# GAT score split into a linear and a relu part in a graph-network kernel: source shares as extra table columns, pair sums read from PSUM

## The reference

```
xl = x @ Wl + bl                       # source side
xr = x @ Wr + br                       # destination side
e = leaky_relu(xl[src] + xr[dst], 0.2) # per edge, 128 numbers
score = einsum('ehc,hc->eh', e, att)   # per edge and head
alpha = softmax of score over the edges of each dst
out[dst] = sum of alpha * xl[src]
```

## Time and profile before

| What | us |
|---|---|
| three runs | 7042.58, 7057.05, 7068.73 |
| median | 7057.05 |
| profiled execution, first to last instruction (span) | 7063.2 |
| first GAT pass, its 832 gathers begin and end within | 2300 to 3440 |
| second GAT pass | 3443 to 4700 |

### The profile page before, as it was taken

The page is one execution under the profiler, slowest core; times in us unless marked ns, Lnnn a source line. Parts: engine busy times, 40 slices in busy tenths (PEclk is TensorE's granted clock), DMA queues, the critical chain, the costliest instruction groups (busy, mean ns, idle before and its releaser), DMA issues. The chain is left out here.

```text
span 7063.2 us, 92210 instructions
## 1 busy us (share of the span) xinstructions
PE 4905.6 (69%) x26319; PEld 4070.8 (58%) x26319; DVE 5007.0 (71%) x14623; ACT 1757.9 (25%) x5241; POOL 4834.6 (68%) x5008
## 2 busy tenths in 40 slices
PE   2555555677666677777688888876888886676766
PEld 2444443566655455555466666656777775666665
DVE  4444433777776688888588878856877774788886
ACT  2333332222222122222122222221222221121121
POOL 3777776777775777777477666627777772777774
PEclk7666676777777888888788888877888886777776
DMA  4544445666665444444454454536766774666665
GB/s 135 170 152 163 160 153 159 206 215 211 209 214 147 149 156 154 152 159 160 106 165 161 153 163 156 170 105 223 245 228 227 238 230 120 222 217 221 226 223 139
DMA packets 408009, 1264.30 MB, mean 179 GB/s; under 512 B 128774, under 2 KB 189958, under 8 KB 321110
## 3 DMA queue, kind: packets, MB, share of 16 engines
q1 hardware_dynamic: 200000, 760.63, 30.1%
q0 software_dynamic: 200240, 492.90, 24.7%
q10 hardware_dynamic: 7270, 4.88, 0.2%
HBM read 1081.15 MB, written 176.88 MB: 178 GB/s over the span
## 5 line engine op out<-in xcount | busy, mean ns | idle before, releaser
L755 POOL DMA_INDIRECT gathered_rows<-table_l,arena x3056 | 2981.2, 976 | 1230.3 <-issue 906.8
L1313 PE MATMUL ps<-weighted_rows,onehot 128*128 128x136 f32 (+2 forms) x8320 | 1547.6, 342 | 646.0 <-DVE acc L1165 641.3
L1313 PEld LDWEIGHTS ps<-weighted_rows,onehot 128*128 128x128 f32 x8320 | 1360.0, 241 | 818.3 <-DVE weighted_rows L1154 382.7
L1280 PEld LDWEIGHTS ps<-dst_side,onehot_t 128*128 128x128 f32 x8320 | 1312.3, 234 | 384.1 <-issue 327.0
L755 POOL DMA_INDIRECT gathered_rows<-table_l,src_rel_edges x1120 | 1067.8, 953 | 601.3 <-issue 329.0
L1280 PE MATMUL ps<-dst_side,onehot_t 128*128 x8320 | 1390.1, 322 | 84.6 <-issue 43.3
L1165 DVE TENSOR_TENSOR acc<-acc,ps 128x136 f32 (+2 forms) x4160 | 1186.4, 285 | 121.3 <-PE ps L1313 39.5
L1277 PE MATMUL ps<-gathered_rows,ident 128*128 128x512 f32 x832 | 556.3, 756 | 266.1 <-DMA gathered_rows<-table_l,arena 256.9
L1087 DVE TENSOR_REDUCE scores<-products 128x16 f32<-128x512 f32 (+2 forms) x1040 | 709.0, 682 | 13.3
L878 PE MATMUL ps<-gathered_rows,onehot 128*128 128x128 f32 x1664 | 346.7, 374 | 471.6 <-ACT gathered_rows L815 470.5
L755 POOL DMA_INDIRECT arena<-table_l,src_rel_edges x544 | 517.6, 952 | 178.3 <-issue 159.8
(11 more groups left out here) (314 smaller groups left out, 6233.5 us busy)
## 6 DMA issues: line engine op xcount, KB each, us to landing
onehot_t<-onehots_turned SPq DMA_DIRECT2D x260, 1024.0 KB
onehot<-onehots SPq DMA_DIRECT2D x260, 1024.0 KB, 5.4
onehots<-onehot SPq DMA_DIRECT2D x52, 1024.0 KB, 6.8
onehots_turned<-onehot_t SPq DMA_DIRECT2D x52, 1024.0 KB, 4.3
table_l<-arena SPq DMA_DIRECT2D x50, 1024.0 KB
gathered_rows<-table_l,arena POOLq DMA_INDIRECT x3056, 2.5
segment_flags_sb<-segment_flags SPq DMA_DIRECT2D x1300, 8.2 KB
arena<-type_mask_rows SPq DMA_DIRECT2D x75, 256.0 KB
```

Of the source, the lines that this page charges most:

```text
L755: pool.indirect_dma_start(out=home(v, t // GC)[:, t % GC, :], out_offset=None, in_=table, in_offset=bass.IndirectOffsetOnAxis(ap=index[:, ...
L1280: ins = nc.tensor.matmul(ps[:, BZ + k, g * P:(g + 1) * P], e.ohT[:, u, t * P:(t + 1) * P], kRows[:, bass.ds(bs[t % 8], D)], start=not gat, ...
L1313: ins = nc.tensor.matmul(ps[:, BP + n % 3, at:at + PW], e.oh[:, u, t, :], exvT[:, t, :], start=True, stop=True)
```

## The change

leaky_relu(z, 0.2) is 0.2 z + 0.8 relu(z). The linear part of a score is a sum of a source share and a destination share; the latter is the same for all edges of a destination and leaves the softmax as it is. The source share, 0.2 att·xl per node and head, is made once per node (`linear_share`), and stored in columns 128 to 131 of the table: a row of a GAT table grows from 512 to 528 bytes. Att is scaled by 0.8 once (`scale_att`). In a slot, VectorE now takes max(z, 0) * att straight out of PSUM in one instruction; ScalarE's four copies and VectorE's four multiplications by att go. ScalarE copies the group's linear shares out of the gathered rows (`keep_linear`), and TensorE adds them when it turns the scores: two accumulating matmuls against the identity in place of one transposition. `own_shares` loses one operation over 128 columns and gains one over 1 or 4. The gathered rows' buffers and the projected rows (`xlW`) get the wider pitch.

```diff
+TW = D + 4
-        t2_d = [table(f"table_l2_{n}", (NPAD, D)) for n in range(2)]
+        t2_d = [table(f"table_l2_{n}", (NPAD, TW)) for n in range(2)]
-        rows = sb("gathered_rows", [P, 2, GT * 2 * D])
+        rows = sb("gathered_rows", [P, 2, GT * 2 * TW])
+        linS = sb("linear_shares", [P, GT * 4])
...
-            def keep_pair_sums(s, j):
+            def keep_linear(s, w):
+
                 if gat:
-                    c, k = J * s + j, j % 2
-                    e.z_ready.wait(act, a_no, c + 1)
-                    if not (static(s, 1) and j < 2):
-
-                        e.score_ready.wait(act, a_no, c - 1)
-                    nc.scalar.activation(e.prod[:, k, :], ps[:, BZ + k, :], ACT.Copy).then_inc(e.zc_ready.sem, 1)
+                    e.z_ready.wait(act, a_no, J * (s + 1))
+                    at = (w % buffers) * GT * width
+                    rows = e.rflat[:, at:at + GT * width].rearrange("p (t c) -> p c t", c=width)
+                    nc.scalar.activation(e.linS[:, 0:L].rearrange("p (h t) -> p h t", t=GT), rows[:, D:D + H, :], ACT.Copy)\
+                        .then_inc(e.linear_kept.sem, 1)
...
                 if gat:
-                    e.zc_ready.wait(dve, gat_no, c + 1)
-                    V.scalar_tensor_tensor(e.prod[:, k, :], ps[:, BZ + k, :], 0.2, e.prod[:, k, :], ALU.mult, ALU.max)\
-                        .then_inc(e.prod_ready.sem, 1)
-                    return
...
+                    ins = V.scalar_tensor_tensor(out, z, 0.0, att.unsqueeze(1).to_broadcast([P, GC, D]), ALU.max, ALU.mult)
...
-            def weight_att(s, j):
-                if gat:
-                    e.prod_ready.wait(dve, a_no, J * s + j + 1)
-                    pr = e.prod[:, j % 2, :].rearrange("p (g d) -> p g d", d=D)
-                    V.tensor_tensor(pr, pr, att.unsqueeze(1).to_broadcast([P, GC, D]), ALU.mult).then_inc(e.att_step.sem, 1)
...
-                    nc.tensor.matmul(ps[:, BZ + k, :], e.ident[:, :], home(v, j).rearrange("p g d -> p (g d)"), start=True, stop=False)
+                    nc.tensor.matmul(ps[:, BZ + k, :].rearrange("p (g d) -> p g d", d=D), e.ident[:, :], home(v, j)[:, :, 0:D],
+                                     start=True, stop=False)
...
-                nc.tensor.transpose(scoresP, e.sc[:, 0:L], e.ident[:, :]).then_inc(e.turned_ready.sem, 1)
+                if gat:
+                    nc.tensor.matmul(scoresP, e.sc[:, 0:L], e.ident[:, :], start=True, stop=False)
+                    e.linear_kept.wait(pe, gat_no, s + 1)
+                    nc.tensor.matmul(scoresP, e.linS[:, 0:L], e.ident[:, :], start=False, stop=True).then_inc(e.turned_ready.sem, 1)
+                else:
+                    nc.tensor.transpose(scoresP, e.sc[:, 0:L], e.ident[:, :]).then_inc(e.turned_ready.sem, 1)
...
+    def scale_att(self, dve):
+
+        n = self.layer
+        att = self.e.vecs[:, (n - 1) * D:n * D]
+        dve.wait_ge(self.S["w"], 16 * 5)
+        self.chain.step(dve, self.nc.vector.tensor_scalar(att, att, 0.8, None, ALU.mult))
+
+    def linear_share(self, dve, k, t, H):
+
+        e, S, V = self.e, self.S, self.nc.vector
+        n = self.layer
+        att, own = e.vecs[:, (n - 1) * D:n * D], e.xlW[:, k, D:D + H]
+        dve.wait_ge(S["own_made"], k + 1)
+        if H == 1:
+            ins = V.scalar_tensor_tensor(t, e.xlN[:, k, :], 0.25, att, ALU.mult, ALU.mult, accum_out=own)
+        else:
+            self.chain.step(dve, V.scalar_tensor_tensor(t, e.xlN[:, k, :], 0.25, att, ALU.mult, ALU.mult))
+            ins = V.tensor_reduce(own, t.rearrange("p (h c) -> p h c", h=H), AX, ALU.add)
+        ins.then_inc(S["share_made"], 1)
+        dve.wait_ge(S["share_made"], k + 1)
...
-        sp.wait_ge(S["own_made"], k + 1)
+        sp.wait_ge(S["share_made"], k + 1)
...
-        sp.dma_start(t2[bass.ds(b, 1), :, :].rearrange("b p d -> p (b d)"), e.xlN[:, k, :]).then_inc(S["written"], 16)
+        sp.dma_start(t2[bass.ds(b, 1), :, :].rearrange("b p d -> p (b d)"), e.xlW[:, k, :]).then_inc(S["written"], 16)
...
+            elif d == 15:
+                self.linear_share(dve, k, self.junk, 4)
...
     c.step(dve, V.tensor_tensor(t, e.xlN[:, k, :], e.kN[:, k, :], ALU.add))
-    c.step(dve, V.scalar_tensor_tensor(t, t, 0.2, t, ALU.mult, ALU.max))
     if H == 1:
-        c.step(dve, V.scalar_tensor_tensor(t, t, 1.0, att, ALU.mult, ALU.mult, accum_out=own))
+        c.step(dve, V.scalar_tensor_tensor(t, t, 0.0, att, ALU.max, ALU.mult, accum_out=own))
     else:
-        c.step(dve, V.tensor_tensor(t, t, att, ALU.mult))
+        c.step(dve, V.scalar_tensor_tensor(t, t, 0.0, att, ALU.max, ALU.mult))
         c.step(dve, V.tensor_reduce(own, t.rearrange("p (h c) -> p h c", h=H), AX, ALU.add))
+    c.step(dve, V.tensor_tensor(own, own, e.xlW[:, k, D:D + H], ALU.add))
...
+            elif d == 10:
+                self.linear_share(dve, k, self.t, 1)
```

More of the change, by code:

```diff
@@ L252, in build @@
         env.vecs, env.wts, env.xN, env.sc, env.score_ready = vecs, wts, xN, sc, score_ready
-        env.turned_ready, env.att_step = turned_ready, att_step
-        env.xlN = xlN
-        env.z_ready, env.zc_ready = z_ready, zc_ready
+        env.turned_ready, env.linear_kept, env.linS = turned_ready, linear_kept, linS
+        env.xlN, env.xlW = xlN, xlW
+        env.z_ready = z_ready
         prepare(nc, A, env)
@@ L259, in build @@
                        after=AfterL1(nc, A, env))
-        attention_pass(nc, env, 2, H=4, table=t2_d[0], width=D, index=srcE, scale=1.0, gat=True, spare=None, att=vecs[:, 0:D],
+        attention_pass(nc, env, 2, H=4, table=t2_d[0], width=TW, index=srcE, scale=1.0, gat=True, spare=None, att=vecs[:, 0:D],
                        after=AfterGat(nc, A, env))
-        attention_pass(nc, env, 3, H=1, table=t2_d[1], width=D, index=srcE, scale=1.0, gat=True, spare=None, att=vecs[:, D:2 * D],
+        attention_pass(nc, env, 3, H=1, table=t2_d[1], width=TW, index=srcE, scale=1.0, gat=True, spare=None, att=vecs[:, D:2 * D],
                        after=AfterGats(nc, A, env))
@@ L1017, in exp_columns, with slot @@
                 nc.scalar.activation(exvH[:, :, :, hs], exE, ACT.Copy).then_inc(e.excol_ready.sem, 1)
-            def slot(s, w, qw, cur=True, chain=True, weigh=True, ahead=True):
+            def slot(s, w, qw, cur=True, chain=True):
                 u, q = two(w, qw)
@@ L1044, in slot @@
                     exp_columns(s - 1)
-                if cur and ahead:
-                    keep_pair_sums(s + 1, 0)
                 after.act(act, x + 7)
-            keep_pair_sums(0, 0)
             for s in range(ways):
-                slot(s, s, 0, chain=s > 0, weigh=s > 1)
-            turns(slot, ways, NG - 1, ways)
-            slot(NG - 1, (NG - 1) % ways, (NG - 1) // ways, ahead=False)
+                slot(s, s, 0, chain=s > 0)
+            turns(slot, ways, NG, ways)
             slot(NG, NG % ways, NG // ways, cur=False)
@@ L1062, in product @@
                 c, k = J * s + j, j % 2
-                if gat:
-                    e.zc_ready.wait(dve, gat_no, c + 1)
-                    V.scalar_tensor_tensor(e.prod[:, k, :], ps[:, BZ + k, :], 0.2, e.prod[:, k, :], ALU.mult, ALU.max)\
-                        .then_inc(e.prod_ready.sem, 1)
-                    return
                 v, qv = buffer(w, qw)
                 e.z_ready.wait(dve, a_no, c + 1)
-                here[v][j].wait(dve, here_no, 64 * (qv + 1))
+                if not gat:
+                    here[v][j].wait(dve, here_no, 64 * (qv + 1))
                 if not (static(s, 1) and j < 2):
                     e.score_ready.wait(dve, a_no, c - 1)
-                V.tensor_tensor(e.prod[:, k, :].rearrange("p (g d) -> p g d", d=D), home(v, j)[:, :, 0:D],
-                                ps[:, BZ + k, :].rearrange("p (g d) -> p g d", d=D), ALU.mult).then_inc(e.prod_ready.sem, 1)
-            def weight_att(s, j):
+                out = e.prod[:, k, :].rearrange("p (g d) -> p g d", d=D)
+                z = ps[:, BZ + k, :].rearrange("p (g d) -> p g d", d=D)
                 if gat:
-                    e.prod_ready.wait(dve, a_no, J * s + j + 1)
-                    pr = e.prod[:, j % 2, :].rearrange("p (g d) -> p g d", d=D)
-                    V.tensor_tensor(pr, pr, att.unsqueeze(1).to_broadcast([P, GC, D]), ALU.mult).then_inc(e.att_step.sem, 1)
+                    ins = V.scalar_tensor_tensor(out, z, 0.0, att.unsqueeze(1).to_broadcast([P, GC, D]), ALU.max, ALU.mult)
+                else:
+                    ins = V.tensor_tensor(out, home(v, j)[:, :, 0:D], z, ALU.mult)
+                ins.then_inc(e.prod_ready.sem, 1)
             def score(s, j):
-                if gat:
-                    e.att_step.wait(dve, gat_no, J * s + j + 1)
-                else:
-                    e.prod_ready.wait(dve, a_no, J * s + j + 1)
+                e.prod_ready.wait(dve, a_no, J * s + j + 1)
```

(2 more changed lines are left out.)

27 lines of the change are left out of this document (9 added, 18 removed).

## The result

The changed kernel takes 6948.47 us (median of four runs, 6944.25 to 6966.49) against 7059.52 before: a ratio of 0.9848, 95% interval 0.9836 to 0.986. The prediction was 6940, range 6850 to 7000. The profiled execution has a span of 6950.0 us, 113.2 less than before; the sum had 117.

The account below looks back on a forecast made before the run. POOL's gathers were taken to bound the first GAT pass, the slot's own chain the second (VectorE in light slots, TensorE in heavy). Terms 36 + 81 = 117 us off gave 6940 us by the median, range 6850 to 7000.

Parts of the forecast that it names:

- First GAT pass: Without the multiplication by att the long gathers go and the pace becomes that of the pass before: 36 us.
- R3: First GAT pass: POOL gains nothing, long gathers come from another two-input operation or the new product; 6976 us, chance 0.08.
- R4: Whole kernel: no change, as TensorE binds every slot and POOL gains nothing; 7022 us, chance 0.08.
- Second GAT pass: Heavy slots shorten by 0.68 us and light ones by 2.33, mean 1.55 over 52 slots: 81 us.
- TensorE is the later one now, and the slot is 22.36: Light slot, second GAT pass: VectorE's way falls to 21.98 us, TensorE's to 22.36, which sets the slot; gain 2.33.
- The parts costed at nothing: ScalarE's removed copies, the turn's second matmul and the wider rows: no change; node work and saved first steps: net 0.
- R5: Gathers: 528 B rows cost POOL more, deciding at a gather of 1.07 us; 8420 us if instructions double, chance 0.07.
- R1: Second GAT pass: TensorE's clock stays up after shorter idle time, gaining 172 us; kernel 6849 us, chance 0.14.
- R2: Second GAT pass: TensorE binds every slot, so only 0.68 us a slot remain, 35 us; kernel 6986 us, chance 0.15.

Follow-up runs that it names:

- times-one version: The changed kernel with a multiplication by a tile of ones at the four places of the old att step: 7058.97 us, 0.9985 of before.
- second reduction: The changed kernel with the sum over features done twice, unread, at the four places of the old att step: 6998.76 us, 0.9911 of before.

## Why the prediction was right, point by point

**First GAT pass: right.** 38.6 us against 36, the gathers' pace equal to that of the pass before, longest gather 1128 ns against the forecast 1.1 us. Some 4 of the 38.6 may be noise, as the transformer pass also differs by 3.7 us. The cause is shown by the pair of runs: same time on VectorE, one or two inputs in SBUF, 31.0 us apart. The Trainium skill (SBUF — State Buffer, Who interferes with whom) says so: two SBUF inputs contend with a GpSimd instruction that reads SBUF, one does not. The runs agree, 1674 against 1111 ns, and rivals R3 and R4 fall. The evidence of the earlier trace rows was weaker than the prediction took it for: L1065 begins 0.37 us into the gather there, and in the same pass L1080 too left the gathers alone that it met so late (of 32 that it met at 0.3 to 0.4 us none took over 957 ns). The pass as a whole bears the reading out: of 100 gathers that began while L1065 ran, none took over 957 ns; of 79 that began while L1080 ran, 51 took over 1200 ns.

**Second GAT pass: right in direction, the term mis-sized.** 67.3 us against 81. Three things are off. The step that failed is "TensorE is the later one now, and the slot is 22.36". TensorE's way was 22.41 us there, as forecast, but the slot took 24.05. The 2.71 us were subtracted from VectorE's way as if all of it were work. Freed of them, VectorE reached a root that comes when TensorE and ScalarE let it, and stood there for 1.85 us; over 800 us its waits for the root grew from 26.9 to 41.5. That this wait is what the light slots lack is read from the timeline; no run took it away. Heavy slots gained 0.53 us (forecast 0.68), light ones 2.05 (forecast 2.33). Next, the two slots did not stand for the pass: heavy slots took 23.26 us on average before, and the chosen one, with 24.78, was the longest of the 23. The pass has stretches with the node matmuls ahead of the drop, where the forecast for light slots, about 22.4, was met (22.2) and the heavy ones lie well below their 24.1 (22.26), and stretches like the one chosen, where light slots take 24. Last, the whole gain was given to the time on VectorE. By the runs 31.3 us were that time, 24.3 the second SBUF input, and the remaining 11.7 lie between the times-one version and before; the copies, 7.1 by their own run, are a part of them. The loop itself, from weighing over the drop and TensorE's work to the next weighing, is borne out: with TensorE's wait for the drop filled the pass falls to the gathers' pace.

**The total is nearer than its parts.** The two passes gave 105.9 us where the sum had 117. The profiled spans differ by 113.2 only because 7.3 more lie where the sum had nothing; that much is luck.

**The parts costed at nothing: right.** Copies 2.9 and 7.1 us, inside the bounds 0 and 35.7 in 800. Single matmul records of the turn take 278 and 273 ns, as the earlier trace rows, but each of the two matmuls leaves two records a slot where the transposition left one (70 and 34 in 800 us), so their uncovered price was taken somewhat too low. It wasn't paid, as they are hidden:

```profile
L1267 PE MATMUL ps<-ident,scores x70: 272/278/283, 3621.3 to 4386.2; 128*16 128x128 f32 x70
...
L1269 PE MATMUL ps<-ident,linear_shares x70: 272/273/273, 3621.5 to 4386.4; 128*16 128x128 f32 x70
```

The wide table and the node work together cost 0.12% (interval 0.03 to 0.22), and gathers kept their median (944 against 947 ns), so R5 falls: its turning point of 1.07 us is far off.

**The clock (R1).** 0.90 in the second pass, the upper end of the forecast 0.86 to 0.9. The stretches of the light slot that answer:

```profile
3965.62:3972.44 6.82, 6.82 (x21) 4.72 (x21) 6.33 (x21) 0.97 (x3) 4.99 (x7) 0.50 0.23 52
3972.44:3978.00 5.56, 5.56 (x36) 4.28 (x35) 2.18 (x8) 2.46 (x6) 1.79 (x2) 1.00 0.41 84
```

After a wait of 2.02 us TensorE still ran at 0.50, 1.2 GHz. R1's price is not borne out: with the clock at 0.99 the second GAT pass takes 1110.4 us, 74.3 less than before, where R1 had 172; but extra matmuls are in the way there. The range of 6850 to 7000 leaves R1's own 6849 out by 1 us, though the prediction says that it covers it.

**R2, that TensorE binds every slot,** falls with the light slots' 2.05 us.

## What to carry to other kernels

When an instruction is removed, ask what the engine will meet next: if its way held a wait that the work had covered, subtract the work and look for the next releaser, here a square root behind two other engines. Read several slots along a pass before taking one pair for all, as node work that drifts through the slot changes what sets it. And besides thinning the busier engine, look at an engine that stands idle at a fixed place in its order: moving independent work into that wait brought here another 84 us, with no instruction removed.

## What the hardware showed unexpectedly

A gather was stretched where the two-input instruction met its beginning. In the timeline of times one, the multiplication that runs from 0.08 us ahead of the gather makes it 1.42 us, and one that starts 0.21 us into a gather makes it 1.67; one that starts 0.51 us into a gather, and overlaps it for 0.43, leaves it at 0.94. In both stretched ones the gather ends 0.82 us after the multiplication does (2797.43 against 2796.61, 2800.42 against 2799.60), as if it had waited for that end. Few are hit: of the 832 gathers of the pass 70 took over 1.2 us, none with the second reduction, and the pass lengthened by 31.0 us, some 0.04 us a gather.
